# Cross-attention with a gate and RMS norm: the reciprocal root on GpSimd instead of VectorE

## Chip, core and metric

The kernel runs on one core of a Trainium2 chip. The metric is the time of one execution on the device in microseconds (us). The engines are called PE (TensorE, matrix products), DVE (VectorE), ACT (ScalarE), POOL (GpSimd) and SP (SyncE, which issues the DMAs).

## What is computed

For each of B = 8 sequences, with x of 512 x 512 and a memory of 1601 x 256:

```python
memory_proj = einsum('bme,de->bmd', memory, W_mem)
scores = einsum('bnd,bmd->bnm', x, memory_proj) / sqrt(D)          # D = 512
attn = softmax(scores, axis=-1)
memory_context = einsum('bnm,bmd->bnd', attn, memory_proj)
gate_input = concatenate([x, memory_context], axis=-1)
gate = sigmoid(einsum('bnf,df->bnd', gate_input, W_gate) + b_gate)
fused = x + gate * memory_context
out = fused * rsqrt(mean(square(fused), axis=-1) + 1e-6) * norm_w
```

Everything is float32. The last line is the one that the change touches: the factor `rsqrt(mean + eps)`, one number for each of the 512 rows of a sequence.

## The kernel before

**Tiling.** 512 rows of x are NT = 4 tiles of 128 rows; the 1601 rows of memory are MT = 13 tiles, the last of 65 rows. Every large product is done as three products of 32-bit parts (a "hi" and a "lo" part: hi·hi, hi·lo, lo·hi), so each operand tile is split: ACT copies the hi part (line 625), DVE subtracts it to get the lo part (line 828, the helper `lo_part`).

**Stages of one iteration b.** PE does the scores of sequence b (lines 353 to 355 with q and mt), then the gate and context products of sequence b-1, then the x half of the gate product of b, then the weighted sum of memory (lines 514 to 516), in the middle of which it computes the queries of b+1. ACT takes the exponential, the copies and the squares; DVE takes the maxima, the subtractions, the lo parts, the gate arithmetic and the stream transposes that prepare b+1. POOL only adds up the exponentials (`add_p`, line 1145): 12 additions of 128x512 in each iteration, into `psum_rows`.

**Order.** It is written out by hand, engine by engine, with semaphores between them; each engine runs its own list in order. A `wait_ge` holds up everything that stands behind it on its engine. Iteration 0 and iteration 7 are written out, 1 to 6 are a loop.

**The rows' factor.** ACT squares the four tiles of `fused` and leaves the sums in `sq_sum`, a 128x4 tile (line 700, semaphore `squares_done`). In iterations 1 to 7 DVE does `rms(b - 1)` after its last `p_lo`, then the four `output` operations (line 1010, 128x512 each) of sequence b-1, and then, for b+1, the lo parts `q_lo` and `mt_lo` (two each), and `u_lo` (two) of b itself. PE's first score product of b+1 waits for `q_lo` and `mt_lo`. In iteration 7 nothing is prepared: `u_lo` stands right behind the outputs, and PE's gate products of the last sequence wait for it. After that the last sequence is finished in a tail without overlap, with its own `rms(B - 1)`; there ACT (line 821) scales two tiles by `r_rms`, DVE the other two (lines 1125 and 1010), and SP stores them.

`rms` is a chain of 11 DVE operations on 128x4 tiles: the mean plus eps (line 996), a first guess from the bits of the number (line 997), and three Newton steps of three operations (lines 1000 to 1002). Each waits for the one before by the semaphore `newton`.

Of the kernel before, what the change touches and what calls it, by code (L numbers as in the profile page):

```python
# [37 lines left out]
P = 128  # L38
BLOCK = 32
BLOCKS = P // BLOCK  # L40
EPS = 1e-6

RSQRT_MAGIC = float(0x5F3759DF)
NEWTON_STEPS = 3


def xattn_kernel(nc: bass.Bass, x, mem, w, wg, b_gate, norm_w, out):
# [19 lines left out]
    with ExitStack() as ctx:  # L67
# [55 lines left out]
        sq_sum = sb("sq_sum", [P, NT])  # L123
        mean_sq = sb("mean_sq", [P, NT])
        r_rms = sb("r_rms", [P, NT])
        nw_a = sb("nw_a", [P, NT])
        nw_b = sb("nw_b", [P, NT])

        w_raw = x_again[:, :, :].rearrange("p a (k c) -> p (a k) c", c=C)
        wg_raw = [  # L130
# [53 lines left out]
        p_has_lo, xt_has_lo, q_has_lo = sem("p_has_lo"), sem("xt_has_lo"), sem("q_has_lo")  # L184
        u_has_lo, gx_done, r_first, r_done = sem("u_has_lo"), sem("gx_done"), sem("r_first"), sem("r_done")
        z_done, gated, fused_done = sem("z_done"), sem("gated"), sem("fused_done")
        newton, out_done = sem("newton"), sem("out_done")

        normed, tail_done = sem("normed"), sem("tail_done")

        p_added = sem("p_added")

        NEWTON_OPS = 2 + 3 * NEWTON_STEPS

        WT, WG2T, WG1T, V = range(0, 2), range(2, 6), range(6, 10), range(10, 12)

# [426 lines left out]
        def _(act):  # L623
# [192 lines left out]

            act.wait_ge(normed, NT - 1)

            act.wait_ge(newton, NEWTON_OPS * B)
            for j in range(1, NT - 1):  # L820
                nc.scalar.activation(fused[:, j, :], gate[:, j, :], ACT.Copy,
                                     scale=r_rms[:, j : j + 1]).then_inc(tail_done, 1)
# [3 lines left out]
        def _(dve):  # L826
# [154 lines left out]
                nc.vector.tensor_tensor(fused[:, j, :], fused[:, j, :], x_again[:, j % 2, :],  # L981
                                        ALU.add).then_inc(fused_done, 1)

            def rms(b):

                count = [NEWTON_OPS * b]

                def link(instruction):

                    count[0] = count[0] + 1  # L990
                    instruction.then_inc(newton, 1)
                    dve.wait_ge(newton, count[0])


                dve.wait_ge(squares_done, NT * (b + 1))
                link(nc.vector.tensor_scalar(mean_sq[:, :], sq_sum[:, :], 1.0 / D, EPS, ALU.mult, ALU.add))
                link(nc.vector.tensor_scalar(r_rms[:, :].bitcast(I32), mean_sq[:, :].bitcast(I32), -0.5, RSQRT_MAGIC,
                                             ALU.mult, ALU.add))
                for _ in range(NEWTON_STEPS):
                    link(nc.vector.tensor_tensor(nw_a[:, :], r_rms[:, :], mean_sq[:, :], ALU.mult))  # L1000
                    link(nc.vector.scalar_tensor_tensor(nw_b[:, :], nw_a[:, :], -0.5, r_rms[:, :], ALU.mult, ALU.mult))
                    link(nc.vector.scalar_tensor_tensor(r_rms[:, :], nw_b[:, :], 1.5, r_rms[:, :], ALU.add, ALU.mult))

            def scale_by_norm(j):

                dve.wait_ge(fused_done, NT * (B - 1) + j + 1)
# [17 lines left out]
            def iteration(b, first, last):  # L1024
# [12 lines left out]
                if first:  # L1037

                    dve.wait_ge(in_rows, 32)
                    reduce_max(b, first)  # L1040
                    for g in [*WG1T, V[0]]:
                        weights(g)
                    shift(b, 0)
                    shift(b, 1)
                    shift(b, 2)
                    for t in range(MT):
                        for q in SPLIT_BY_SOFTMAX.get(t, []):
                            mem_lo_part(b, q)
                        softmax(b, t, not last)
                        if t == 1:  # L1050
                            weights(V[1])
                        if 1 <= t < 1 + NT:
                            add_bias(b, t - 1, first)
                        transpose_next(b, t, first)
                else:
                    reciprocal(b - 1)
                    gate_input(b - 1, 0)
                    reduce_max(b, first)
                    gate_ctx(b - 1, 0)
                    gate_input(b - 1, 1)  # L1060
                    add_x(b - 1, 0)
                    shift(b, 0)
                    shift(b, 1)
                    shift(b, 2)
                    for t in range(MT):

                        if t in (1, 2):
                            gate_input(b - 1, t + 1)
                        if 3 <= t < 3 + NT:
                            add_bias(b, t - 3, first)  # L1070
                        if t in (0, 2, 4):
                            gate_ctx(b - 1, 1 + t // 2)
                        if t in ADD_AT:
                            add_x(b - 1, ADD_AT.index(t) + 1)
                        for q in SPLIT_BY_SOFTMAX.get(t, []):
                            mem_lo_part(b, q)
                        softmax(b, t, not last)
                        if not last:
                            transpose_next(b, t, first)
                    rms(b - 1)  # L1080
                    for j in range(NT):
                        output(b - 1, j)
                if not last:
# [36 lines left out]
            gate_ctx(B - 1, NT - 1)  # L1120
            add_x(B - 1, NT - 1)
            scale_by_norm(NT - 2)
            rms(B - 1)

            nc.vector.tensor_scalar(fused[:, 0, :], gate[:, 0, :], r_rms[:, 0:1], None, ALU.mult).then_inc(out_done, 1)
            output(B - 1, NT - 1)

# [2 lines left out]
        def _(pool):  # L1130
            def add_p(b, t, first):
# [12 lines left out]
                    a = psum_rows[0:r, :]  # L1144
                nc.gpsimd.tensor_tensor(psum_rows[0:r, :], a, p_tmp[0:r, t % TMP_RING, :], ALU.add).then_inc(p_added, 1)  # L1145

            nc.gpsimd.memset(ident[:, :], 0.0).then_inc(cleared, 1)
            pool.wait_ge(cleared, 1)
            nc.gpsimd.affine_select(out=ident[:, :], in_=ident[:, :], compare_op=ALU.not_equal, fill=1.0, base=0,
                                    pattern=[[-1, P]], channel_multiplier=1).then_inc(ready_ident, 1)  # L1150
# [2 lines left out]
            with pool.Fori(1, B) as b:  # L1153
                for t in range(1, MT):
                    add_p(b, t, False)


# [24 lines left out]
```

## Time and profile before

| what | us |
|---|---|
| median of 3 runs | 568.89 |
| lowest, highest | 568.46, 569.97 |
| span of the profiled execution | 567.1 |
| first to last score product of one loop iteration (148.48 to 215.53) | 67.05 |

The span is counted from the first to the last instruction on the engines; the run's time has 1.8 us more, which lie outside it. The page of the profile gives, for each engine, the busy time as a share of the span. PE's rows are modelled at their ends: a 128x512 product is shown as 0.39 us long, though the next one starts 0.23 us after it, so PE's pace is read from start to start. All times below are counted from the start of the span.

### The profile page before, as it was taken

Reading aid. Unit: us, or ns where it says so; the run is one execution under the profiler, and the core shown is the slowest. Engines: PE = TensorE matmul, PEld = TensorE weight load, DVE = VectorE, ACT = ScalarE, POOL = GpSimd, SP = SyncE. Lnnn points to the kernel's source line nnn. Section 1 sums busy time; section 2 is a strip of 40 time slices with the busy share of each in tenths; the row PEclk is TensorE's granted clock in tenths of the full one; section 3 lists DMA queues with packets and bytes.
Section 4 is the critical chain, followed back from the end, with each engine's and each line's share of the span. In section 5 each row is a group of like instructions: output and inputs, shape, how many; then the busy total and the mean of one; then the engine's idle time right before and its main releaser. Section 6 shows DMA issues by size and latency. Waiting matters only on the chain.

```text
span 567.1 us, 8588 instructions
## 1 busy us (share of the span) xinstructions
PE 541.8 (96%) x2416; PEld 436.3 (77%) x2416; DVE 511.6 (90%) x847; ACT 336.1 (59%) x633; POOL 134.2 (24%) x102
## 2 busy tenths in 40 slices
PE   6999999999999999999999999999999999999992
PEld 5877788877788777878788777887778777787882
DVE  3789959999899999899988998999988999889976
ACT  3666637665567655585466664666556754657534
POOL 0005500244002520055101550024300352005600
PEclk9999999999999999999999999999999999999997
DMA  9965151520853109521285115652095210210033
GB/s 235 271 102 113 52 134 42 99 69 26 186 137 93 37 3 237 102 74 37 83 176 102 55 37 146 130 98 78 1 214 125 77 37 33 97 33 29 1 113 111
DMA packets 89457, 54.24 MB, mean 96 GB/s; under 512 B 52696, under 2 KB 79840, under 8 KB 89440
## 3 DMA queue, kind: packets, MB, share of 16 engines
q1 hardware_dynamic: 89296, 53.51, 39.4%
q10 hardware_dynamic: 144, 0.52, 0.3%
q8 instruction: 8, 0.13, 0.1%
q14 instruction: 9, 0.07, 0.0%
HBM read 45.63 MB, written 8.39 MB: 95 GB/s over the span
## 4 chain that ended last, share of the span: by engine, by line
DVE 41%; PE 39%; issue 15%; ACT 2%; DMA 1%; DVEq 0%; ACTq 0%
PE bank L353 12%; DVE p_lo L828 11%; PE bank L355 11%; PE bank L354 11%; DVE s L869 6%; DVE bank L934 5%; DVE fused L974 3%; DVE gate L895 3%; DVE fused L981 2%; DVE xt_lo L828 2%; ACT fused L686 2%; DVE gate L924 2%; DVE fused L1010 1%; DVE q_lo L828 1%; PE bank L534 1%
## 5 line engine op out<-in xcount | busy, mean ns | idle before, releaser
L1145 POOL TENSOR_TENSOR psum_rows<-psum_rows,p_tmp 128x512 f32<-128x512 f32 (+1 forms) x88 | 122.6, 1393 | 94.1 <-ACT p_tmp L663 93.0
L828 DVE TENSOR_TENSOR p_lo<-p_tmp,p_hi 128x512 fp32r<-128x512 f32 (+1 forms) x104 | 92.4, 890 | 4.8 <-ACT p_hi L625 4.8
L663 ACT ACTIVATE p_tmp<-s 128x512 f32<-128x512 f32 (+1 forms) x104 | 65.3, 628 | 43.6 <-DVE s L869 43.0
L514 PE MATMUL bank<-p_hi,mem_hi 128*128 128x512 f32 (+1 forms) x208 | 81.8, 393 | 2.3 <-DVE p_lo L828 2.3
L1145 POOL TENSOR_TENSOR psum_rows<-p_tmp 128x512 f32<-128x512 f32 x8 | 10.8, 1354 | 308.7 <-ACT p_tmp L663 308.7
L353 PE MATMUL bank<-q_hi,mt_hi 128*128 128x512 f32 (+1 forms) x208 | 82.3, 396 | 1.1 <-DVE mt_lo L828 1.0
L355 PE MATMUL bank<-q_hi,mt_lo 128*128 128x512 f32 (+1 forms) x208 | 81.2, 390 | 0.0
L354 PE MATMUL bank<-q_lo,mt_hi 128*128 128x512 f32 (+1 forms) x208 | 81.2, 390 | 0.0
L515 PE MATMUL bank<-p_lo,mem_hi 128*128 128x512 f32 (+1 forms) x208 | 81.1, 390 | 0.0
L516 PE MATMUL bank<-p_hi,mem_lo 128*128 128x512 f32 (+1 forms) x208 | 80.9, 389 | 0.0
L625 ACT ACTIVATE s<-bank 128x512 f32<-128x512 f32 (+1 forms) x104 | 62.1, 597 | 22.0 <-PE bank L355 21.6
L869 DVE TENSOR_TENSOR s<-s,bank 128x512 f32<-128x512 f32 (+1 forms) x104 | 68.6, 673 | 0.0
L840 DVE TENSOR_TENSOR run<-run,s 128x512 f32<-128x512 f32 (+1 forms) x88 | 60.0, 681 | 8.0 <-ACT s L625 5.8
L625 ACT ACTIVATE p_hi<-p_tmp 128x512 fp32r<-128x512 f32 (+1 forms) x104 | 63.5, 617 | 0.0
L353 PE MATMUL bank<-wg1t_hi,xt_hi 128*128 128x512 f32 x128 | 51.9, 405 | 5.9 <-DVE gate L895 5.9
L354 PE MATMUL bank<-wg1t_lo,xt_hi 128*128 128x512 f32 x128 | 50.0, 391 | 0.0
L355 PE MATMUL bank<-wg1t_hi,xt_lo 128*128 128x512 f32 x128 | 49.9, 390 | 0.0
L514 PEld LDWEIGHTS bank<-p_hi,mem_hi 128*128 128x128 f32 (+1 forms) x208 | 39.0, 188 | 13.2 <-DVE p_lo L828 5.3
L353 PEld LDWEIGHTS bank<-q_hi,mt_hi 128*128 128x128 f32 (+1 forms) x208 | 38.2, 184 | 12.2 <-issue 3.1
L625 ACT ACTIVATE mt_hi<-bank 128x512 fp32r<-128x512 f32 (+1 forms) x56 | 30.2, 554 | 28.7 <-PE bank L355 28.7
L516 PEld LDWEIGHTS bank<-p_hi,mem_lo 128*128 128x128 f32 (+1 forms) x208 | 39.0, 188 | 8.3
L355 PEld LDWEIGHTS bank<-q_hi,mt_lo 128*128 128x128 f32 (+1 forms) x208 | 38.2, 184 | 9.2
(91 smaller groups left out, 1040.8 us busy)
## 6 DMA issues: line engine op xcount, KB each, us to landing
mem_raw<-in_ctx_dram SPq DMA_DIRECT2D x48, 256.0 KB, 2.9
mem_blocks<-in_ctx_dram SPq DMA_DIRECT2D x32, 272.0 KB
x_raw<-in_x_dram SPq DMA_DIRECT2D x32, 256.0 KB, 4.6
x_again<-in_x_dram SPq DMA_DIRECT2D x32, 256.0 KB, 2.8
out_dram<-fused SPq DMA_DIRECT2D x32, 256.0 KB, 2.1
mem_blocks<-in_ctx_dram SPq DMA_DIRECT2D x28, 128.0 KB, 5.5
gate<-in_L_xattn_W_gate_dram SPq DMA_DIRECT2D x2, 512.0 KB, 5.8
fused<-in_L_xattn_W_gate_dram SPq DMA_DIRECT2D x2, 512.0 KB, 7.4
```

Source lines behind the costliest of these rows:

```text
L353: nc.tensor.matmul(dst, a_hi, b_hi, start=(start and i == 0), stop=False)
L354: nc.tensor.matmul(dst, a_hi, b_lo, start=False, stop=False)
L355: last = nc.tensor.matmul(dst, a_lo, b_hi, start=False, stop=(stop and i == n - 1))
L514: nc.tensor.matmul(dst, mem_hi[0:r, t, cs], p_hi[0:r, t, :], start=(t == 0), stop=False)
L515: nc.tensor.matmul(dst, mem_hi[0:r, t, cs], p_lo[0:r, t % LO_RING, :], start=False, stop=False)
L516: last = nc.tensor.matmul(dst, mem_lo[0:r, t, cs], p_hi[0:r, t, :], start=False, stop=(t == MT - 1))
L625: return nc.scalar.activation(dst, src, ACT.Copy)
L663: nc.scalar.activation(p_tmp[0:r, t % TMP_RING, :], s[0:r, t, :], ACT.Exp, scale=float(D) ** -0.5).then_inc(exp_done, 1)
L828: return nc.vector.tensor_tensor(dst, src, hi.bitcast(F32), ALU.subtract)
L840: nc.vector.tensor_tensor(run[0:r, :], a, s[0:r, t, :], ALU.max).then_inc(run_done, 1)
L869: nc.vector.tensor_tensor(s[0:r, t, :], s[0:r, t, :], bank[MAX_BANK][0:r, :], ALU.subtract).then_inc(shifted, 1)
L1145: nc.gpsimd.tensor_tensor(psum_rows[0:r, :], a, p_tmp[0:r, t % TMP_RING, :], ALU.add).then_inc(p_added, 1)
```

## The change

The chain on DVE is taken out. POOL gets an `rms` of three operations on 128x4 tiles: `sq_sum` times a tile that holds 1/D, plus a tile that holds eps, to the power of a tile that holds -0.5. Each waits for the one before (`mean_done`, `guarded`), and the last one counts up `rms_done`. It stands on POOL behind the twelve `add_p` of iterations 1 to 7, and once more at the end. DVE waits for `rms_done` where its chain stood, in front of the outputs, and ACT waits for `rms_done` in the tail. The three constant tiles are filled by POOL at the start, between the clearing of `ident` and the `affine_select` that makes it the identity.

```diff
-            def rms(b):
-                count = [NEWTON_OPS * b]
-                def link(instruction):
-                    count[0] = count[0] + 1
-                    instruction.then_inc(newton, 1)
-                    dve.wait_ge(newton, count[0])
-                dve.wait_ge(squares_done, NT * (b + 1))
-                link(nc.vector.tensor_scalar(mean_sq[:, :], sq_sum[:, :], 1.0 / D, EPS, ALU.mult, ALU.add))
-                link(nc.vector.tensor_scalar(r_rms[:, :].bitcast(I32), mean_sq[:, :].bitcast(I32), -0.5, RSQRT_MAGIC,
-                                             ALU.mult, ALU.add))
-                for _ in range(NEWTON_STEPS):
...
@@ DVE, iteration b @@
-                    rms(b - 1)
+                    dve.wait_ge(rms_done, b)
                     for j in range(NT):
                         output(b - 1, j)
@@ DVE, tail @@
-            rms(B - 1)
+            dve.wait_ge(rms_done, B)
@@ ACT, tail @@
-            act.wait_ge(newton, NEWTON_OPS * B)
+            act.wait_ge(rms_done, B)
@@ POOL @@
+            def rms(b):
+                pool.wait_ge(squares_done, NT * (b + 1))
+                nc.gpsimd.tensor_tensor(mean_sq[:, :], sq_sum[:, :], one_in_d[:, :], ALU.mult).then_inc(mean_done, 1)
+                pool.wait_ge(mean_done, b + 1)
+                nc.gpsimd.tensor_tensor(mean_sq[:, :], mean_sq[:, :], eps_rows[:, :], ALU.add).then_inc(guarded, 1)
+                pool.wait_ge(guarded, b + 1)
+                nc.gpsimd.tensor_tensor(r_rms[:, :], mean_sq[:, :], minus_half[:, :], ALU.pow).then_inc(rms_done, 1)
             nc.gpsimd.memset(ident[:, :], 0.0).then_inc(cleared, 1)
+            nc.gpsimd.memset(minus_half[:, :], -0.5).then_inc(ready_half, 1)
+            nc.gpsimd.memset(one_in_d[:, :], 1.0 / D).then_inc(ready_half, 1)
+            nc.gpsimd.memset(eps_rows[:, :], EPS).then_inc(ready_half, 1)
+            pool.wait_ge(ready_half, 3)
...
             with pool.Fori(1, B) as b:
                 for t in range(1, MT):
                     add_p(b, t, False)
+                rms(b - 1)
+            rms(B - 1)
```

On DVE, at the end of a loop iteration, this stood in a row before (the register steps compute the loop's semaphore values; the first rows are the last preparation for b+1 and the last `p_lo`):

```order
L950 STREAM_TRANSPOSE bank<-mem_blocks 128x512
L828 TENSOR_TENSOR p_lo<-p_tmp,p_hi 65x512
L996 TENSOR_SCALAR mean_sq<-sq_sum 128x4
L992 ISA
L997 TENSOR_SCALAR r_rms<-mean_sq 128x4
L992 REGISTER_ALU
L1000 TENSOR_TENSOR nw_a<-r_rms,mean_sq 128x4
L992 REGISTER_ALU
L1001 SCALAR_TENSOR_TENSOR nw_b<-nw_a,r_rms 128x4
L992 REGISTER_ALU
L1002 SCALAR_TENSOR_TENSOR r_rms<-nw_b,r_rms 128x4
L992 REGISTER_ALU
```

and this stands at the same place now:

```order
L948 STREAM_TRANSPOSE bank<-mem_blocks 128x512
L826 TENSOR_TENSOR p_lo<-p_tmp,p_hi 65x512
L988 SCALAR_TENSOR_TENSOR fused<-fused,r_rms,norm_rows 128x512 x4
L903 ISA
L826 TENSOR_TENSOR q_lo<-bank,q_hi 128x512
L903 REGISTER_ALU
L826 TENSOR_TENSOR q_lo<-bank,q_hi 128x512
L842 ISA
L826 TENSOR_TENSOR mt_lo<-bank,mt_hi 128x512
```

The eleven operations between the last `p_lo` and the four outputs are gone, and nothing else moved on DVE (its line numbers are smaller by 2 to 22).

On POOL, at the end of a loop iteration, this stood before:

```order
L1145 TENSOR_TENSOR psum_rows<-psum_rows,p_tmp 65x512
L1153 REGISTER_ALU
L1153 COMPARE_AND_BRANCH
L67 UNCONDITIONAL_BRANCH
```

and this stands there now, with the copy for the last sequence behind the loop's branch:

```order
L1124 TENSOR_TENSOR psum_rows<-psum_rows,p_tmp 65x512
L1128 REGISTER_ALU
L1129 TENSOR_TENSOR mean_sq<-sq_sum,one_in_d 128x4
L1131 TENSOR_TENSOR mean_sq<-mean_sq,eps_rows 128x4
L1133 TENSOR_TENSOR r_rms<-mean_sq,minus_half 128x4
L1145 REGISTER_ALU
L1145 COMPARE_AND_BRANCH
L1129 TENSOR_TENSOR mean_sq<-sq_sum,one_in_d 128x4
L1131 TENSOR_TENSOR mean_sq<-mean_sq,eps_rows 128x4
L1133 TENSOR_TENSOR r_rms<-mean_sq,minus_half 128x4
L65 UNCONDITIONAL_BRANCH
```

The three small operations came in behind the last addition of the iteration; no addition moved.

## Rows read from the trace of the kernel before

**Rows 1.** The page, part 1: busy us (share of the span) xinstructions.

```profile
PE 541.8 (96%) x2416; PEld 436.3 (77%) x2416; DVE 511.6 (90%) x847; ACT 336.1 (59%) x633; POOL 134.2 (24%) x102
```

**Rows 2.** Waits: engine line waited for: us in total, times, longest us.

```profile
PE bank L353 <- DVE mt_lo L828: 1.0, 5, 0.2
...
PEld bank L353 <- DVE mt_lo L828: 0.6, 1, 0.6
```

**Rows 3.** Timeline of PE at two turns: start, length, instruction [idle before <-releaser].

```profile
81.29 0.39 PE L516 MATMUL bank<-p_hi,mem_lo 65*128 65x512 f32 x1
81.52 0.40 PE L353 MATMUL bank<-q_hi,mt_hi 128*128 128x512 f32 x1
...
147.87 0.39 PE L516 MATMUL bank<-p_hi,mem_lo 65*128 65x512 f32 x1
148.48 0.49 PE L353 MATMUL bank<-q_hi,mt_hi 128*128 128x512 f32 x1 [0.21 <-DVE mt_lo L828]
148.81 0.40 PE L354 MATMUL bank<-q_lo,mt_hi 128*128 128x512 f32 x1
```

**Rows 4.** Timeline of DVE before the second turn.

```profile
141.07 0.66 DVE L828 TENSOR_TENSOR p_lo<-p_tmp,p_hi 65x512 fp32r<-65x512 f32 x1
141.66 0.14 DVE L996 TENSOR_SCALAR mean_sq<-sq_sum 128x4 f32<-128x4 f32 x1
...
143.81 2.74 DVE L1010 SCALAR_TENSOR_TENSOR fused<-fused,r_rms,norm_rows 128x512 f32<-128x512 f32 x4
...
147.66 1.28 DVE L828 TENSOR_TENSOR mt_lo<-bank,mt_hi 128x512 fp32r<-128x512 f32 x2
```

**Rows 5.** Timeline of ACT, same stretch.

```profile
140.51 0.19 ACT L700 ACTIVATION_READ_ACCUMULATOR squares_out<-fused 128x1 f32 x1
...
144.69 1.08 ACT L625 ACTIVATE mt_hi<-bank 128x512 fp32r<-128x512 f32 x2
```

**Rows 6.** Timelines of ACT, POOL and DVE: POOL's last addition of iteration 1.

```profile
135.93 0.63 ACT L663 ACTIVATE p_tmp<-s 65x512 f32<-65x512 f32 x1
...
136.72 1.45 POOL L1145 TENSOR_TENSOR psum_rows<-psum_rows,p_tmp 65x512 f32<-65x512 f32 x1 [0.88 <-ACT p_tmp L663]
...
137.53 1.19 DVE L828 TENSOR_TENSOR p_lo<-p_tmp,p_hi 128x512 fp32r<-128x512 f32 x1
```

**Rows 7.** Timeline of the start; then POOL's additions by line: duration ns min/median/max.

```profile
0.35 0.10 POOL L1170 MEMSET const-uint8-127<- 128x1 uint8 x1
...
1.19 0.29 POOL L1149 TENSOR_SCALAR_AFFINE_SELECT ident<-ident 128x128 f32<-128x128 f32 x1 [0.24 <-POOL ident L1147]
...
5.26 3.66 PE L364 MATMUL bank<-ident,x_raw 128*128 128x128 f32 x16 [5.26 <-DMA x_raw<-in_x_dram]
...
L1145 POOL TENSOR_TENSOR psum_rows<-psum_rows,p_tmp x88: 1286/1329/1796, 48.0 to 536.3; 128x512 f32<-128x512 f32 x80, 65x512 f32<-65x512 f32 x8
```

**Rows 8.** Timelines of DVE, ACT and PE at the end of iteration 7.

```profile
538.82 1.28 DVE L828 TENSOR_TENSOR p_lo<-p_tmp,p_hi 128x512 fp32r<-128x512 f32 x2
...
539.47 0.19 ACT L700 ACTIVATION_READ_ACCUMULATOR squares_out<-fused 128x1 f32 x1
...
542.19 2.74 DVE L1010 SCALAR_TENSOR_TENSOR fused<-fused,r_rms,norm_rows 128x512 f32<-128x512 f32 x4
...
543.81 1.29 ACT L625 ACTIVATE u_hi<-bank 128x512 fp32r<-128x512 f32 x2 [4.15 <-PE bank L516]
...
544.30 0.95 PE L449 MATMUL bank<-ones,psum_rows 128*128 128x1 f32 x8
545.59 0.50 PE L353 MATMUL bank<-v_hi,u_hi 128*128 128x512 f32 x1 [0.34 <-DVE u_lo L828]
```

**Rows 9.** Timeline of the tail.

```profile
559.59 0.19 ACT L700 ACTIVATION_READ_ACCUMULATOR squares_out<-fused 128x1 f32 x1
559.81 0.17 DVE L996 TENSOR_SCALAR mean_sq<-sq_sum 128x4 f32<-128x4 f32 x1 [0.19 <-ACT squares_out L700]
...
562.05 1.33 ACT L821 ACTIVATE fused<-gate,r_rms 128x512 f32<-128x512 f32 x2 [2.27 <-DVE r_rms L1002]
```

More of the change, by code:

```diff
@@ L41 @@
 EPS = 1e-6
-RSQRT_MAGIC = float(0x5F3759DF)
-NEWTON_STEPS = 3
 def xattn_kernel(nc: bass.Bass, x, mem, w, wg, b_gate, norm_w, out):
@@ L125, in xattn_kernel @@
         r_rms = sb("r_rms", [P, NT])
-        nw_a = sb("nw_a", [P, NT])
-        nw_b = sb("nw_b", [P, NT])
+        minus_half = sb("minus_half", [P, NT])
+        one_in_d = sb("one_in_d", [P, NT])
+        eps_rows = sb("eps_rows", [P, NT])
         w_raw = x_again[:, :, :].rearrange("p a (k c) -> p (a k) c", c=C)
@@ L186, in xattn_kernel @@
         z_done, gated, fused_done = sem("z_done"), sem("gated"), sem("fused_done")
-        newton, out_done = sem("newton"), sem("out_done")
+        mean_done, guarded, rms_done, out_done = sem("mean_done"), sem("guarded"), sem("rms_done"), sem("out_done")
+        ready_half = sem("ready_half")
         normed, tail_done = sem("normed"), sem("tail_done")
         p_added = sem("p_added")
-        NEWTON_OPS = 2 + 3 * NEWTON_STEPS
         WT, WG2T, WG1T, V = range(0, 2), range(2, 6), range(6, 10), range(10, 12)
@@ L982, in add_x @@
                                         ALU.add).then_inc(fused_done, 1)
-            def rms(b):
-                count = [NEWTON_OPS * b]
-                def link(instruction):
-                    count[0] = count[0] + 1
-                    instruction.then_inc(newton, 1)
-                    dve.wait_ge(newton, count[0])
-                dve.wait_ge(squares_done, NT * (b + 1))
-                link(nc.vector.tensor_scalar(mean_sq[:, :], sq_sum[:, :], 1.0 / D, EPS, ALU.mult, ALU.add))
-                link(nc.vector.tensor_scalar(r_rms[:, :].bitcast(I32), mean_sq[:, :].bitcast(I32), -0.5, RSQRT_MAGIC,
-                                             ALU.mult, ALU.add))
-                for _ in range(NEWTON_STEPS):
-                    link(nc.vector.tensor_tensor(nw_a[:, :], r_rms[:, :], mean_sq[:, :], ALU.mult))
-                    link(nc.vector.scalar_tensor_tensor(nw_b[:, :], nw_a[:, :], -0.5, r_rms[:, :], ALU.mult, ALU.mult))
-                    link(nc.vector.scalar_tensor_tensor(r_rms[:, :], nw_b[:, :], 1.5, r_rms[:, :], ALU.add, ALU.mult))
             def scale_by_norm(j):
```

## Prediction

> **What bounds the kernel now.** I read the page first. PE is busy for 96% of the span and DVE for 90% [rows 1]. With two engines so full, taking work off DVE pays only where DVE releases PE, so I looked next at the list of waits for PE waiting on what stands behind the chain. PE's first score product waits for DVE's `mt_lo` at six turns of the iteration: five times in the list as a product, once as its weight load [rows 2]. These are the six turns from iteration 1 on to 7. The turn from iteration 0 to 1 has no chain before it, and there PE goes from the last weighted product to the first score product in 0.23 us, its ordinary pace [rows 3]. At the next turn, where DVE has done its chain, the same step takes 0.61 us and the following one 0.33 (the first product after a pause is slow), so 0.94 instead of 0.46: **0.48 us lost at each of six turns** [rows 3].
>
> The timeline of DVE shows why. The chain runs from 141.66 to 143.81, 2.15 us; from there on outputs, `q_lo` and `mt_lo` follow without idle time, and the first half of `mt_lo` is what PE waits for [rows 4]. DVE comes too late by 0.4 us only, however: what the chain costs PE at a turn is less than a quarter of its length.
>
> The chain stands at two more places. In iteration 7, `u_lo` behind the outputs releases PE, which waits 0.34 us [rows 8]. In the tail nothing covers it: from the end of the squares (559.78) to ACT's first use of the factor (562.05) are 2.27 us [rows 9].
>
> **What the change removes.** At eight places a chain of about 2.15 us on DVE. At the six turns at most 0.48 us of it can be won. ACT is no obstacle: `mt_hi` is done at 145.77, earlier than `mt_lo` would start even if it moved up by 1.8 us [rows 4, 5].
>
> **What it adds: POOL's three operations.** No row shows a small arithmetic operation on POOL, so I bound each. Below: filling a 128x1 tile took 0.10 us. Above, for the multiplication and the addition: the `affine_select` on 128x128, a 32 times larger tile, took 0.29 us [rows 7]. I take 0.20 for each, the middle. The gap between two dependent POOL operations was 0.24 us before that `affine_select` [rows 7]; I take 0.20, since a part of it belongs to the start. From the end of an ACT operation to a POOL operation that waits for it pass 0.16 us (136.56 to 136.72) [rows 6]; I use 0.15.
>
> The power is the unknown of this case. POOL has no operation of this kind in the trace. Below it is no shorter than the filling, 0.10. Above, the nearest row is the largest that POOL has, 1.80 us for an addition of 128x512 [rows 7], 128 times as many elements; a power computed in software may cost many times an addition for each element, so this end isn't safe. Between ends so far apart I take the geometric middle, sqrt(0.10 x 1.80) = 0.42, say **0.44 us**, and keep d for it.
>
> **The shared port.** DVE's `p_lo` of 0.66 us takes 1.19 when POOL's addition is running, and ends 0.55 after that addition ends (138.17 to 138.72): it has waited for POOL, not been slowed by it [rows 4, 6]. In the Trainium skill, "SBUF — State Buffer", section "Who interferes with whom", an operation of VectorE with two SBUF inputs and a GpSimd operation that reads SBUF exclude each other; by that rule, the trace agrees. So POOL's small operations can also wait for `p_lo`, and I count this against the change.
>
> **When the factor is ready, at a turn.** Squares end at 140.70 [rows 5]. POOL's additions of this iteration ended at 138.17 [rows 6], so POOL is free. Multiplication from 140.85 to 141.05. The addition could start at 141.25, but `p_lo` holds the port until about 141.66 [rows 4]: 141.66 to 141.86. Power from 142.06, end 142.06 + d, DVE starts 0.10 later. With d = 0.44 the outputs start at 142.60 instead of 143.81, **1.21 us earlier**; without the port 0.41 more. The turn needs only 0.48. So each turn wins min(0.48, 1.65 - d) = 0.48, in sum **2.88 us**. What is late next there is PE itself, which has its own weighted products until then. Downstream nothing new comes up: the scores are paced by PE, and the softmax stage starts from PE's transposes, so the whole iteration shifts.
>
> **Iteration 7.** Squares end at 539.66, `p_lo` holds the port until about 540.08 [rows 8]. Multiplication to 540.28, addition to 540.68, power from 540.88, outputs at 540.98 + d = 541.42 instead of 542.19: 0.77 us. PE can use 0.34, since its row sums last until 545.25, and `u_hi` is ready then [rows 8]: **0.34 us**.
>
> **Tail.** 559.78 + 0.15 + 0.20 + 0.20 + 0.20 + 0.20 = 560.73 for the start of the power, then d and 0.10 to ACT: 561.27 instead of 562.05 [rows 9], **0.78 us** (1.32 with all durations at their lower ends and gaps unchanged).
>
> **Start.** Three more fillings on POOL, 0.10 us each, at most 0.3 us before the identity. The identity was ready at 1.48 and PE's first transpose waited for x until 5.26 [rows 7]: hidden by 3.8 us of DMA, nothing.
>
> **Sum:** 2.88 + 0.34 + 0.78 = 4.00 us off the profiled span of 567.1. The median stands 1.8 us above that span and I carry this over: 568.89 - 4.0 = **564.9 us**.
>
> **As a function of d:** six turns of min(0.48, 1.65 - d), iteration 7 with min(0.34, 1.21 - d), the tail with 1.22 - d. The gain falls under 0.3% of the time (1.7 us, about what a measurement of this kernel can tell from no change) at d = 1.33, is zero at 1.54, and is a loss of 1.7 us at 1.75. Beyond, every us of d costs 8 us.
>
> **Rivals.**
> - **The power is slow.** DVE then sits in front of its outputs, with `q_lo`, `mt_lo` and `u_lo` queued behind, and PE waits for these. The place is the same eight waits; it decides from d = 1.54 on. At the upper end from rows, d = 1.80: 6 x 0.15 + 0.59 + 0.58 = 2.1 us lost, 571.0 us. For it speaks that no row bounds a power on POOL; against it, that there are only four elements in a partition.
> - **The turns don't pay.** PE starts the scores earlier, and the softmax stage, where DVE is full, gives it back by a longer wait. DVE's own work after the turn is not shortened, and its 90% speak for it; that PE releases the reduction at that stage's head speaks against it. Then only 0.34 + 0.78 remain: 567.8 us, within 0.3%.
> - **The first power loads code.** No row shows POOL loading code: the accumulating additions, from the first at 48.0 us on, lie between 1286 and 1796 ns [rows 7], which speaks against it; but none of them is a power. If the first power took the 1.8 us of my upper end and the others 0.44, the first turn would lose 0.15 instead of gaining 0.48: 565.5 us. The Trainium skill, "GPSIMD Engine Reference", section "2.1 Instruction dispatch", states about 6 us for the first call into freshly loaded code; by an estimate from that page the first turn would be late by 4.7 us and the time 570.1. No run here shows such a load.
>
> **How the numbers follow.** The power below 1.33 us and the turns paying: 0.64, all of it faster by over 0.3%. The turns don't pay: 0.13, within. A first power that costs several us once: 0.03, within. The power above 1.33: 0.20, of which 0.05 lie between 1.33 and 1.75, within, and 0.15 above, slower. So faster 0.64, same 0.21, slower 0.15. Low end: all of POOL at its lower bounds gives 4.00 + 0.54 = 4.5, with the runs' spread below the median (0.4) 563.9, say 563.8. High end: 571.0, the power at 1.80; above it lie about 0.14.
>
> **What would show it right or wrong.** The power's row, below 1.3 us; DVE's idle time before the first output, about 142.6 - 141.7 = 0.9 us a turn, released by POOL; PE from last weighted to first score product in 0.23 us at all seven turns, and no wait for `mt_lo`; a loop iteration of 66.6 instead of 67.05 us; the tail from squares to ACT's scaling 1.5 us. Wrong: a wait of DVE for POOL above 2.15 us, or PE's turns closed with the iteration still at 67.05.

## The result, and the profile after

The changed kernel takes 565.17 us (median of 4 runs, 564.69 to 565.91) against 569.43 us for the kernel before beside it (4 runs, 568.46 to 571.36): a ratio of 0.9918 with a 95% interval of 0.9896 to 0.9941. The prediction said 564.9 in a range of 563.8 to 571.0, faster. The profiled execution of the changed kernel has a span of 564.0 us.

The page after (line numbers are 2 to 22 smaller than before on the engines). First part 1, then part 4, the shares of the chain that ended last:

```profile
PE 540.6 (96%) x2416; PEld 436.7 (77%) x2416; DVE 499.7 (89%) x759; ACT 336.1 (60%) x633; POOL 152.5 (27%) x129
...
PE 55%; DVE 29%; issue 12%; ACT 2%; DMA 1%; DVEq 0%; ACTq 0%; POOLq 0%; POOL 0%
```

DVE has 88 operations less, PE the same work as in [rows 1]. PE now holds 55% of the chain, where the page of before had DVE 41% and PE 39%.

The waits of the changed kernel (engine line waited for: us in total, times, longest us). These are three of those that are new; PE's wait for `mt_lo` of [rows 2] isn't in the list any more:

```profile
POOL mean_sq L1129 <- ACT squares_out L698: 33.1, 8, 17.9
...
DVE fused L988 <- POOL r_rms L1133: 8.7, 7, 1.5
...
ACT fused L819 <- POOL r_rms L1133: 1.7, 1, 1.7
```

A turn is the step from one iteration's last weighted product on PE to the first score product of the next. The second one that has a factor before it, for each engine of the changed kernel (start, length, instruction [idle before <-releaser]):

```profile
207.80 0.20 POOL L1129 TENSOR_TENSOR mean_sq<-sq_sum,one_in_d 128x4 f32<-128x4 f32 x1 [2.60 <-ACT squares_out L698]
208.08 0.74 POOL L1131 TENSOR_TENSOR mean_sq<-mean_sq,eps_rows 128x4 f32<-128x4 f32 x1
208.90 1.03 POOL L1133 TENSOR_TENSOR r_rms<-mean_sq,minus_half 128x4 f32<-128x4 f32 x1
...
208.10 0.66 DVE L826 TENSOR_TENSOR p_lo<-p_tmp,p_hi 65x512 fp32r<-65x512 f32 x1
209.97 2.74 DVE L988 SCALAR_TENSOR_TENSOR fused<-fused,r_rms,norm_rows 128x512 f32<-128x512 f32 x4 [1.21 <-POOL r_rms L1133]
...
214.91 0.39 PE L514 MATMUL bank<-p_hi,mem_lo 65*128 65x512 f32 x1
215.14 0.40 PE L351 MATMUL bank<-q_hi,mt_hi 128*128 128x512 f32 x1
215.37 0.40 PE L352 MATMUL bank<-q_lo,mt_hi 128*128 128x512 f32 x1
```

Read it beside [rows 3] and [rows 4]. From the start of the last `p_lo` to the outputs pass 1.87 us instead of 2.74, though DVE stands idle for 1.21 of them. PE goes on in 0.23 + 0.23 us, its pace, where it took 0.61 + 0.33 before. The three POOL operations take 0.20, 0.74 and 1.03 us, and DVE's idle time of 1.21 us is what the prediction put at 0.9.

The end of the chain in the tail, to be read beside [rows 9]:

```profile
557.06 0.19 ACT L698 ACTIVATION_READ_ACCUMULATOR squares_out<-fused 128x1 f32 x1
557.32 0.20 POOL L1129 TENSOR_TENSOR mean_sq<-sq_sum,one_in_d 128x4 f32<-128x4 f32 x1 [17.92 <-ACT squares_out L698]
557.60 0.20 POOL L1131 TENSOR_TENSOR mean_sq<-mean_sq,eps_rows 128x4 f32<-128x4 f32 x1
557.88 1.01 POOL L1133 TENSOR_TENSOR r_rms<-mean_sq,minus_half 128x4 f32<-128x4 f32 x1
...
558.98 1.33 ACT L819 ACTIVATE fused<-gate,r_rms 128x512 f32<-128x512 f32 x2 [1.74 <-POOL r_rms L1133]
```

From the end of the squares (557.25) to ACT's scaling are 1.73 us instead of 2.27.

So that the start of a run, where the arrival of x moves everything by a few tenths, doesn't enter, the table counts from the first score product of iteration 1 (81.52 before, 81.81 after). "Six turns" is the stretch from there to iteration 7's first score product, six loop iterations with their turns.

| stretch, us | before | after | won |
|---|---|---|---|
| six turns (iterations 1 to 6) | 402.23 | 399.89 | 2.34 |
| iteration 7, to the gate products of the last sequence | 61.84 | 61.32 | 0.52 |
| squares of the last tile to the scaling | 2.27 | 1.73 | 0.54 |
| first score product of iteration 1 to the end | 485.6 | 482.2 | 3.4 |

The start took 0.29 us longer in the profiled execution of the changed kernel, and 3.4 - 0.3 = 3.1 is the difference of the spans. PE's first transposes waited for x until 5.42 instead of 5.26, not for the identity.

### The profile page after: what moved, and what is told of

It is laid out like the page before. It is cut to its first block, busy times and chain, and to the rows that moved or that the text cites. A ratio compares the mean times of both kernels' runs of the same rounds, so it can differ in the third digit from the quotient of the medians.

```text
span 564.0 us, 8469 instructions
## 1 busy us (share of the span) xinstructions
PE 540.6 (96%) x2416; PEld 436.7 (77%) x2416; DVE 499.7 (89%) x759; ACT 336.1 (60%) x633; POOL 152.5 (27%) x129
## 4 chain that ended last, share of the span: by engine, by line
PE 55%; DVE 29%; issue 12%; ACT 2%; DMA 1%; DVEq 0%; ACTq 0%; POOLq 0%; POOL 0%
PE bank L351 14%; PE bank L353 13%; PE bank L352 13%; DVE p_lo L826 7%; DVE s L867 5%; DVE bank L932 5%; PE bank L512 4%; PE bank L513 3%; PE bank L514 3%; DVE fused L972 3%; DVE gate L893 2%; DVE xt_lo L826 2%; ACT fused L684 2%; DVE gate L922 2%; DVE fused L979 2%
## 5 line engine op out<-in xcount | busy, mean ns | idle before, releaser
L1124 POOL TENSOR_TENSOR psum_rows<-psum_rows,p_tmp 128x512 f32<-128x512 f32 (+1 forms) x88 | 126.0, 1432 | 94.2 <-ACT p_tmp L661 93.1
```

## The experiments

**Theory:** what counts is only the moment at which the factor is ready, at six turns with a cap (PE's own pace), in iteration 7 and in the tail. **Rivals:** the relief of VectorE's busy time pays, wherever the factor is computed; GpSimd's added operations take part of the gain back; the tail carries nearly everything. Each run was measured beside the kernel before on the same chip; there were two chips, so that runs are compared by their ratio or by their traces. "To the end" is the stretch of the last line of the table above, in the profiled execution.

### A later factor

```diff
+                nc.gpsimd.tensor_tensor(r_first_pow[:, :], mean_sq[:, :], minus_half[:, :], ALU.pow).then_inc(pow_once, 1)
+                pool.wait_ge(pow_once, b + 1)
                 nc.gpsimd.tensor_tensor(r_rms[:, :], mean_sq[:, :], minus_half[:, :], ALU.pow).then_inc(rms_done, 1)
```

> The changed kernel with the power computed twice in a row, the second waiting for the first, at all eight places. In the changed kernel's trace the power takes 1.02 us and the gap before it 0.08, so the factor is 1.10 us later. Theory (only the moment at which the factor is ready counts): from the start of the last p_lo to the outputs 1.86 + 1.10 = 2.96 us at a turn, where the chain on VectorE needed 2.74; PE waits for mt_lo again, 0.2 us a turn longer than before the change; 0.5 us are lost in iteration 7 and 0.56 in the tail. In sum 2.4 us slower than the kernel before, about 571.8, that is 6.6 above the changed kernel. Rival (relief of VectorE's busy time is what pays, since VectorE has no more work than in the changed kernel): within 1 us of the changed kernel's 565.2 but for the tail, so below 567.5.

Measured: 571.14 us against 569.23, ratio 1.0027 (1.0014 to 1.0041). With 1.1 us more of a wait on an engine that is three quarters idle, the whole gain is gone and more. The six turns take 403.52 us, 1.29 more than before (0.2 a turn expected), and PE takes 0.81 us from the last weighted to the first score product. The waits in its trace:

```profile
DVE fused L989 <- POOL r_rms L1136: 16.3, 7, 2.6
...
PE bank L352 <- DVE mt_lo L827: 2.4, 6, 0.4
```

DVE has exactly the work of the changed kernel here and the result is slower than the kernel before, so the relief of DVE isn't what pays: that rival falls. To the end, this profiled execution lost 3.9 us, 1.5 more than the theory's 2.4; that part has another cause, at the end of this document. In the medians the loss is 1.9.

### Loop or tail alone

Set against the changed kernel, both put VectorE's chain of 11 operations back at one kind of place; GpSimd's operations for that place are taken out.

```diff
@@ GpSimd in the iterations only: DVE, tail @@
-            dve.wait_ge(rms_done, B)
+            rms(B - 1)
@@ GpSimd in the tail only: DVE, iteration b @@
-                    dve.wait_ge(rms_done, b)
+                    rms(b - 1)
```

> GpSimd's three operations in iterations 1 to 7, VectorE's chain in the tail. Theory: the tail falls back from 1.73 to 2.27 us between the squares and the scaling, 0.54 us above the changed kernel, about 565.7; 3.7 us faster than before. Rival (most of the gain is in the exposed tail and the turns give theirs back in the softmax stage): about 568.

> VectorE's chain in iterations 1 to 7, GpSimd's three operations in the tail alone. Theory: 0.54 us faster than the kernel before, about 568.9, with PE waiting for mt_lo at the turns as before. Rival (the tail carries the gain): about 566.

Measured: in the iterations only 565.46 us (ratio 0.9931, 0.9909 to 0.9952), in the tail only 568.97 (0.9999, 0.9984 to 1.0015). To the end they won 3.2 and 0.4 us; together that is 3.6, where the change won 3.4. Turns in the iterations only: 399.59 us; in the tail only: 402.30, as before. The gain sits where PE waited for `mt_lo`. That the tail carries it is refuted.

### No factor at all

This kernel leaves the factor out: `r_rms` is filled with 1 once at the start, and nobody computes it or waits for it.

```diff
-                    dve.wait_ge(rms_done, b)
+                    dve.wait_ge(squares_done, NT * b)
...
-                rms(b - 1)
-            rms(B - 1)
```

> The changed kernel without the factor: it is a constant 1, nobody computes it and nobody waits for it; the rest is unchanged. It shows what is to be had at all. Theory: a turn can win no more than 0.48 us, iteration 7 no more than 0.34, the tail 2.2: 5.4 us under the kernel before, about 564.0, so only some 1.3 us under the changed kernel, nearly all of it in the tail. Rival (VectorE's readiness still holds back the turns of the changed kernel, or GpSimd's small operations disturb it through the shared port): further 0.1 us a turn or more, 563.3 or lower, and a loop iteration under 66.6 us.

Measured: 563.52 us, ratio 0.9895 (0.9874 to 0.9916). The six turns take 399.54 us: **the floor of a loop iteration with its turn is 66.59 us**, and the change, at 66.65, is all but on it. 0.44 us is what it can win over 67.04, and not 0.48: PE's step from the last weighted to the first score product was 0.61 us only at the turn of [rows 3], and at the six turns 0.61, 0.60, 0.58, 0.56, 0.57 and 0.52. The last of them, in the kernel before:

```profile
483.23 0.39 PE L516 MATMUL bank<-p_hi,mem_lo 65*128 65x512 f32 x1
483.75 0.50 PE L353 MATMUL bank<-q_hi,mt_hi 128*128 128x512 f32 x1
```

Against the pace of 0.23 that is 2.06 us in sum, 0.34 a turn. The 0.10 of a first product after a pause falls into the stretch of the six turns five times, 0.5 us; the sixth stands in the line of iteration 7. Together 2.6 us, where this run won 2.69. To the end 5.4 us are won, 2.0 more than by the change, most of it in the tail, where the scaling follows the squares without a wait.

### A shorter chain, left on VectorE

```diff
-NEWTON_STEPS = 3
+NEWTON_STEPS = 2
```

> The kernel before with two Newton steps instead of three, all on VectorE, GpSimd without the new work: a shorter chain, 8 operations of 0.197 us instead of 11, 0.59 us less. The factor is a little less exact. Theory (only the moment at which mt_lo is ready counts, whoever computes the factor): PE was late by 0.38 us at a turn, 0.59 covers that, so the six turns win what the run without a factor won, 0.44 us each; iteration 7 wins 0.34, the tail 0.59: 3.6 us faster than before, about 565.6, the same as the move to GpSimd. Rival (the work has to leave VectorE): 3/11 of the chain goes, so about 3/11 of the gain, near 568.2.

Measured: 565.04 us, ratio 0.9922 (0.9906 to 0.9938), as the change. Turns 399.62, to the end 3.7 us won. Cutting 0.59 us of 2.15 won everything that the turns had to give: PE was late by 0.38 us. This is the strongest run for the theory. Nothing left DVE here, and the rival's 568.2 is missed by 3 us.

### What the added operations cost others

VectorE's chain stays in use, and POOL does its three operations besides, into tiles of its own that nobody reads. DVE's wait for them stands behind the outputs.

```diff
                     for j in range(NT):
                         output(b - 1, j)
+                    dve.wait_ge(rms_done, b)
...
                 add_p(b, t, False)
+                rms(b - 1)
+            rms(B - 1)
```

> The kernel before, VectorE's chain in use, and GpSimd's three operations done besides into tiles that nobody reads. Measures what the added operations cost others by themselves. Theory: at most 0.1 us a turn by the shared port, 0 to 0.6 us slower than before, iteration 67.05 to 67.15 us. Rival (the added operations disturb VectorE by more, and this ate a part of the gain): 1.5 us or more slower.

Measured: 569.34 us, ratio 1.0004 (0.9991 to 1.0018); turns 402.28 us against 402.23. The operations cost others nothing that shows, though the second one waits itself for DVE's `p_lo`:

```profile
274.75 0.20 POOL L1157 TENSOR_TENSOR pm_sq<-sq_sum,one_in_d 128x4 f32<-128x4 f32 x1 [2.60 <-ACT squares_out L706]
275.03 0.74 POOL L1159 TENSOR_TENSOR pm_sq<-pm_sq,eps_rows 128x4 f32<-128x4 f32 x1
275.85 1.03 POOL L1161 TENSOR_TENSOR pr_rms<-pm_sq,minus_half 128x4 f32<-128x4 f32 x1
```

### The price of a power

```diff
+            for i, (n, op) in enumerate(((4, ALU.add), (4, ALU.pow), (4, ALU.pow), (1, ALU.pow), (16, ALU.pow), (64, ALU.pow), (64, ALU.add))):
+                nc.gpsimd.tensor_tensor(probe_o[:, 0:n], probe_a[:, 0:n], probe_e[:, 0:n], op).then_inc(probe, 1)
+                pool.wait_ge(probe, 3 + i)
```

> The changed kernel with a probe at the start, where GpSimd is idle: an addition on 128x4, then powers on 128x4, 128x4 again, 128x1, 128x16 and 128x64, then an addition on 128x64, each waiting for the one before. The time of the whole says nothing. If the power's cost is fixed for an instruction, all powers take about 1.0 us. If it goes by the element: 0.2 + 0.2 for each column, so 0.4 on 128x1, 1.0 on 128x4, 3.5 on 128x16, 13 on 128x64. If the first power loads code, the first of the two on 128x4 is longer than the second by a microsecond or more.

One execution, the profiled one (564.94 us). POOL's timeline in its first microseconds, cut at the probe's single operations (the longer rows of a view merge operations that follow one another):

```profile
1.85 0.20 POOL L1148 TENSOR_TENSOR probe_o<-probe_a,probe_e 128x4 f32<-128x4 f32 x1
2.13 1.02 POOL L1148 TENSOR_TENSOR probe_o<-probe_a,probe_e 128x4 f32<-128x4 f32 x1
...
2.13 2.11 POOL L1148 TENSOR_TENSOR probe_o<-probe_a,probe_e 128x4 f32<-128x4 f32 x2
...
4.95 2.91 POOL L1148 TENSOR_TENSOR probe_o<-probe_a,probe_e 128x16 f32<-128x16 f32 x1
...
7.93 10.55 POOL L1148 TENSOR_TENSOR probe_o<-probe_a,probe_e 128x64 f32<-128x64 f32 x1
```

and its groups by shape, where the power on 128x1 stands alone:

```profile
L1148 POOL TENSOR_TENSOR probe_o<-probe_a,probe_e 128x1 f32<-128x1 f32 x1 | 0.5, 548 | 0.1
```

The addition on 128x4 takes 0.20 us. The first power takes 1.02, and the second of the pair ends 2.11 us after the first began, so it takes 1.0 as well: no loading of code shows. Powers on 1, 4, 16 and 64 columns take 0.55, 1.02, 2.91 and 10.55 us. Between 1 and 64 columns that is 10.0 / 63 = 0.16 us a column, and 0.39 us whatever the width. By the column both expected pictures were off: a fixed price is refuted, and the slope is 0.16, not 0.2, above a larger base.

### Versions that beat both

Two operations instead of three, and then also the tail's factor in two parts, the first three tiles ahead of the last:

```diff
-                nc.gpsimd.tensor_tensor(mean_sq[:, :], sq_sum[:, :], one_in_d[:, :], ALU.mult).then_inc(mean_done, 1)
-                pool.wait_ge(mean_done, b + 1)
-                nc.gpsimd.tensor_tensor(mean_sq[:, :], mean_sq[:, :], eps_rows[:, :], ALU.add).then_inc(guarded, 1)
+                nc.gpsimd.tensor_tensor(mean_sq[:, :], sq_sum[:, :], eps_rows[:, :], ALU.add).then_inc(guarded, 1)
...
-            nc.gpsimd.memset(eps_rows[:, :], EPS)
+            nc.gpsimd.memset(eps_rows[:, :], D * EPS)
...
+                    nc.vector.tensor_scalar(norm_rows[:, :], norm_rows[:, :], float(D) ** 0.5, None, ALU.mult)
# split tail
+            dve.wait_ge(rms_done, B + 1)
             output(B - 1, NT - 1)
...
-            rms(B - 1)
+            for i, c in enumerate((slice(0, NT - 1), slice(NT - 1, NT))):
+                pool.wait_ge(squares_done, NT * (B - 1) + c.stop)
+                nc.gpsimd.tensor_tensor(mean_sq[:, c], sq_sum[:, c], eps_rows[:, c], ALU.add).then_inc(guarded, 1)
+                pool.wait_ge(guarded, B + i)
+                nc.gpsimd.tensor_tensor(r_rms[:, c], mean_sq[:, c], minus_half[:, c], ALU.pow).then_inc(rms_done, 1)
```

> The changed kernel, improved: 1/D is folded into norm_w (times sqrt(D), once at the start) and D*eps into the constant, so the mean needs no multiplication and two operations are left; in the tail the factors of the first three tiles are computed before the last tile's squares are done, and the last one alone afterwards. Theory: the turns are at their floor and win nothing; the tail's last output ends 1.45 + 0.75 us after the squares instead of 1.73 + 1.33: 0.86 us faster than the changed kernel, about 564.3. Rival (the end is set by the stores or by POOL, not by the factor): the same as the changed kernel.

> The changed kernel once more, beside the two improved ones on the same chip. 0.992 of the time before, 565 to 565.6.

> The changed kernel with two operations on GpSimd instead of three (1/D folded into norm_w, D*eps into the constant), the tail not split. Theory: the turns are at their floor; the tail ends 0.28 us earlier (one operation of 0.20 and one gap of 0.08): 0.3 us under the changed kernel. Rival (the turns still have something to win): 0.5 us or more.

> Two operations and the split tail once more, beside the changed kernel on the same chip. 0.9 to 1.2 us under the changed kernel, as between the earlier runs.

| kernel | median us | ratio to before, interval | six turns | to the end, won |
|---|---|---|---|---|
| changed, again | 565.00 | 0.9916, 0.9897 to 0.9935 | 399.71 | 3.6 |
| two operations | 563.96 | 0.9906, 0.9886 to 0.9926 | 399.48 | 4.1 |
| two operations, split tail | 563.99 | 0.9906, 0.9888 to 0.9924 | 399.65 | 4.7 |
| the same, second time | 563.88 | 0.9900, 0.9880 to 0.9920 | 399.63 | 4.8 |

The split tail is 1.1 to 1.2 us under the change in the trace and 1.0 to 1.1 in the median (0.86 expected; 0.80 of it are the tail, the rest is spread). The first of the split tail's two rows was measured on the other chip than the three other rows. Two operations alone are 0.5 under the change in the trace: 0.28 are the tail (1.46 us instead of 1.74 of waiting), 0.23 the turns, which vary by as much; in the median it is 1.0, more than the 0.3 expected, and part of that is its start (first score product of iteration 1 at 80.54 instead of 81.37). The split tail:

```profile
555.74 1.18 POOL L1153 TENSOR_TENSOR r_rms<-mean_sq,minus_half 128x3 f32<-128x3 f32 x1
556.18 0.19 ACT L698 ACTIVATION_READ_ACCUMULATOR squares_out<-fused 128x1 f32 x1
556.89 0.18 POOL L1151 TENSOR_TENSOR mean_sq<-sq_sum,eps_rows 128x1 f32<-128x1 f32 x1
...
557.01 1.33 ACT L819 ACTIVATE fused<-gate,r_rms 128x512 f32<-128x512 f32 x2 [0.65 <-POOL r_rms L1153]
557.16 0.69 POOL L1153 TENSOR_TENSOR r_rms<-mean_sq,minus_half 128x1 f32<-128x1 f32 x1
...
557.88 0.75 DVE L988 SCALAR_TENSOR_TENSOR fused<-fused,r_rms,norm_rows 128x512 f32<-128x512 f32 x1 [0.44 <-POOL r_rms L1153]
```

The last squares end at 556.37 and the last output 2.26 us later, as expected (2.20); ACT scales its two tiles in the meantime. The first power is still running when the last squares are done, and holds the second one's operations up by 0.4 to 0.5 us.

### Why the kernel before varies more

The median won 4.3 us, the span of the profiled executions 3.1. All 10 runs of the changed kernel lie between 564.22 and 565.91; the kernel before, in its many runs beside the experiments, between 568.05 and 571.49, and its profiled execution (567.1, so 568.9) stands in the lower half. The mean granted clock of each execution, on record for the 68 of the kernel before beside the experiments, divides them:

| mean granted clock | executions | median us | lowest, highest |
|---|---|---|---|
| 0.992 | 31 | 570.3 | 569.54, 571.49 |
| 0.993 to 0.996 | 37 | 568.85 | 568.05, 569.87 |

So most of the one-sided spread goes with the clock: the second group spreads over 1.8 us, as the changed kernel does (1.7), and that kernel has no execution at 0.992. The last run moves one output behind the two `u_lo` in iteration 7, to test what may bring the lower clock:

```diff
-                    for j in range(NT):
+                    for j in range(NT - 1 if last else NT):
                         output(b - 1, j)
...
+                if last:
+                    output(b - 1, NT - 1)
```

> The kernel before, with its chain on VectorE at all places, and only this moved: in iteration 7 the fourth output stands behind the two u_lo instead of in front. u_lo is then ready as early as u_hi allows and PE pauses no longer before the gate products of the last sequence; the turns and the tail stay as they were. Theory A: only the pause goes, 0.3 to 0.5 us. Theory B: in about half the executions of the kernel before the pause is followed by some microseconds at the lower of TensorE's two clocks (the executions with a mean granted clock of 0.992 are 1 to 2 us longer than those with 0.994), and with the pause this goes too: 1.0 to 1.3 us off the median, no execution at 0.992 and none above 569.5. By A alone the executions stay spread up to 571.

Measured: 568.67 us against 568.95, ratio 0.9987 (0.9976 to 0.9999). The pause is gone (PE starts the gate products 0.88 us after its row sums began, in [rows 8] it was 1.29). None of its 12 executions has the mean clock 0.992, which 4 of the 17 beside it have. One is at 570.06 all the same, and the 1.0 to 1.3 us of theory B aren't in the median; with only 4 of 17 at the lower clock beside it, the median before, 568.95, had little of it to lose. By this run alone B is not settled. The other runs speak for it: among the executions whose clock is on record, 41 of the 104 of kernels that pause there (before, power twice, tail only, both chains) are at 0.992 or below, and none of the 58 of kernels without this pause. Against it stands that the tail-only kernel, which pauses as the kernel before does, has one in 12. Only the power-twice kernel was profiled with such a stretch (at the end of this document).

The profiled execution of this last run shows a second cause that neither theory had. The turn from iteration 1 to 2:

```profile
136.59 3.21 POOL L1147 TENSOR_TENSOR psum_rows<-psum_rows,p_tmp 65x512 f32<-65x512 f32 x1 [0.89 <-ACT p_tmp L663]
...
137.41 0.66 DVE L828 TENSOR_TENSOR p_lo<-p_tmp,p_hi 128x512 fp32r<-128x512 f32 x1
138.62 1.72 DVE L981 TENSOR_TENSOR fused<-fused,x_again 128x512 f32<-128x512 f32 x1
...
147.74 0.39 PE L516 MATMUL bank<-p_hi,mem_lo 65*128 65x512 f32 x1
148.90 0.49 PE L353 MATMUL bank<-q_hi,mt_hi 128*128 128x512 f32 x1 [0.77 <-DVE mt_lo L828]
```

In [rows 6] the addition was done after 1.45 us and `p_lo`, which began 0.81 us after it, waited for it and took 1.19. Here `p_lo` began 0.82 us after the addition and went through in 0.66; the addition lasted 3.21 us, and the next DVE operation with two SBUF inputs waited 1.1 us for its end. DVE lost 0.5 us, and PE took 1.16 us for the step at the turn instead of 0.61. At three turns of the six the last addition was longer than 1.9 us and PE's step too long (1.16, 1.10 and 1.08 us): 1.6 us in sum. In the changed kernel's profile the last addition was long three times too (2.00, 3.20 and 2.64 us). The second of them:

```profile
270.38 3.20 POOL L1124 TENSOR_TENSOR psum_rows<-psum_rows,p_tmp 65x512 f32<-65x512 f32 x1 [0.90 <-ACT p_tmp L661]
...
272.40 1.73 DVE L979 TENSOR_TENSOR fused<-fused,x_again 128x512 f32<-128x512 f32 x1
...
281.57 0.39 PE L514 MATMUL bank<-p_hi,mem_lo 65*128 65x512 f32 x1
281.81 0.49 PE L351 MATMUL bank<-q_hi,mt_hi 128*128 128x512 f32 x1
282.14 0.39 PE L352 MATMUL bank<-q_lo,mt_hi 128*128 128x512 f32 x1
```

and cost 0.1 us there, a first product of 0.33 instead of 0.23. The 0.87 us by which DVE is earlier cover 0.38 of lateness and the 0.5 of the lost race.

A long addition isn't always dear, though. The kernel with GpSimd in the tail only has one of 2.63 us, and PE's step at the turn that follows is 0.60 us, as at its other turns:

```profile
202.96 2.63 POOL L1149 TENSOR_TENSOR psum_rows<-psum_rows,p_tmp 65x512 f32<-65x512 f32 x1 [0.90 <-ACT p_tmp L666]
...
204.97 1.18 DVE L984 TENSOR_TENSOR fused<-fused,x_again 128x512 f32<-128x512 f32 x1
...
214.11 0.39 PE L519 MATMUL bank<-p_hi,mem_lo 65*128 65x512 f32 x1
214.71 0.49 PE L356 MATMUL bank<-q_hi,mt_hi 128*128 128x512 f32 x1 [0.21 <-DVE mt_lo L831]
```

What counts is the row of the DVE operation that waits. In all 14 traces, at the last addition of iterations 1 to 6, it is 1.16 to 1.20 us long when the addition takes 1.45 or 2.64, and 1.72 to 1.75 us when it takes 2.0 or 3.2: DVE waits 0.5 or 1.1 us, and its row ends 0.55 us after the addition's each time. The longer wait is there at 9 of these 84 turns, three of them in the last run and none in the profiled execution of the kernel before.

The widths of the runs fit this in part: the kernels whose PE waits for `mt_lo` spread over 1.9 (power twice), 3.6 (tail only), 2.7 (both) and 2.5 us (this one), those with slack there over 0.4 to 1.7 (0.4 iterations only, 0.7 no factor, 1.2 two Newton steps, 1.4 two operations, 1.7 the changed kernel). The first four have 12 executions each and the others 6 to 10, which alone makes a range wider. The tail-only kernel reaches 571.20 at a mean clock of 0.993, so the clock isn't all of it there; how often an execution loses the race wasn't measured beyond the one profiled of each kernel.

## Why the prediction was right

**What bounds.** Right. PE's lateness of 0.38 us at the turn and the cap of 0.48 a turn were read from PE's start-to-start times [rows 3]; the run with two Newton steps and the one without a factor reached a floor of 66.6 us a loop iteration, from either side. The turns won 0.39 us each, 2.34 in sum, where 2.88 was said. One turn had been read for all six, and it was the latest of them: the lateness is 0.34 us on average, not 0.38, and one of the six slow first products falls into the line of iteration 7. That makes 2.6 of the 2.88. The remaining 0.2 went with the long additions, which used up the slack at two turns (first products of 0.33 us); these weren't in the sum.

**The power.** This is the term that was mis-sized: 1.02 us, where 0.44 was taken. It lay between the bounds 0.10 and 1.80. The forecast stood all the same, since by its own function the turns are at their cap up to d = 1.17. Half a microsecond more of power would have used up the slack: the outputs came 0.87 us earlier, and PE needed 0.38 of it.

**The gaps and small operations.** 0.20 us for the multiplication and the addition was right (0.20, 0.20 in the tail). The gap between dependent operations was 0.08, not 0.20. In the tail the errors partly cancel: the power is 0.57 longer, two gaps 0.24 shorter, POOL's start after ACT 0.08 shorter: 1.73 us where 1.49 was said, a gain of 0.54 instead of 0.78.

**The port.** Right, and at each of the six turns: the second operation takes 0.74 to 0.76 us instead of 0.20, ending 0.06 us after `p_lo` (208.82 and 208.76). Outputs were said to start 1.21 us earlier with d = 0.44; by its function, 1.65 - d, the power of 1.02 would give 0.63, and 0.87 was measured, the difference being the shorter gaps and the addition's early end behind `p_lo`, 0.06 us instead of 0.20.

**Iteration 7.** 0.52 us where 0.34 was said. 0.41 of it is at the place itself: PE goes on 0.88 us after the start of its row sums, where it was 1.29, and the prediction let them hold it up for 0.95. The other 0.11 is the faster first score product of iteration 7, the sixth of the turns' 0.10.

**Sum and median.** 3.4 us of 4.0 came in the trace. The medians moved by more, 4.3: of the four executions before, two (569.97 and 571.36) lie higher than any of the 37 at the higher mean clock. Against the median of those 37, 568.85, the ten executions of the changed kernel win 3.8 us. That this kernel would have none at the lower clock wasn't seen beforehand. The hit at 564.9 is in part luck: the sum was 0.6 us too large, and the changed kernel's profiled execution, 565.91, is the slowest of its four, so that the median, 565.17, came nearer to the forecast than the trace.

**Rivals.** The slow power was the right one to fear: at 1.02 + 1.10 (power twice) the kernel is 1.9 us slower than before. The formula with d = 2.12 gave 6 x 0.47 + 0.91 + 0.90 = 4.6; the shorter gaps make it less. The turns paid. No loading of code shows: in the probe the first and the second power take the same.

## What to carry to other kernels

Before moving work off a full engine, measure by how much the engine that waits for it is late: here 0.38 us of a chain of 2.15 decided nearly everything, and three ways of taking 0.6 to 2.15 us out of the chain (another engine, a shorter formula, nothing at all) came out within 0.1 us a turn of each other. A step that is late by a little also passes on every small disturbance; slack of half a microsecond nearly made the lost races disappear. Read every turn of a loop before multiplying: one read for six made the sum 0.2 us too large. And an exposed tail is worth splitting: what can be computed for the first tiles need not wait for the last.

## What the runs showed of the hardware

**A power on GpSimd** took 0.39 us and 0.16 us for each column of 128 in the probe (0.55, 1.02, 2.91 and 10.55 us for 1, 4, 16 and 64 columns), where an addition on 4 columns took 0.20. In the split tail, with DVE at work beside it, 3 columns took 1.18 us and 1 column 0.69, more than the 0.87 and 0.55 of that formula; the cause wasn't traced. A dependent POOL operation started 0.08 us after the one before, and POOL's multiplication 0.07 us after the squares, where an addition started 0.16 us after the exponential.

**At the shared port DVE loses 0.5 or 1.1 us, and which of the two isn't seen in the start times; nor is the longer addition always the dearer one.** An addition that begins 0.81 or 0.82 us ahead of `p_lo` gave one time 1.45 us with `p_lo` waiting 0.5, the other time 3.21 us with `p_lo` going through and the next operation with two SBUF inputs waiting 1.1; one of 2.63 us cost DVE 0.5 as well, one of 2.00 us in the changed kernel cost it 1.1. In the Trainium skill, "SBUF — State Buffer", section "Who interferes with whom", the shared port pair is an exclusive lock, and the order of issue decides who blocks. That the one waits for the other's end agrees with the traces (at all 84 turns of the 14 traces the waiting DVE row ends 0.55 us after the addition's); the order of issue does not show in them, since the addition's row begins first each time. POOL's rows may begin before the port is asked for; that wasn't measured.

**A pause of PE can be followed by the lower clock.** With the power computed twice, PE stood 0.84 us for `u_lo` after its row sums. The products that follow, and the clock in this stretch (PE, PEld, DVE, ACT and POOL busy, then the granted clock):

```profile
546.81 0.50 PE L352 MATMUL bank<-v_hi,u_hi 128*128 128x512 f32 x1 [0.84 <-DVE u_lo L827]
...
548.21 0.63 PE L354 MATMUL bank<-v_hi,u_lo 128*128 128x512 f32 x1
548.63 0.63 PE L352 MATMUL bank<-wt_hi,u_hi 128*128 128x512 f32 x1
...
546.50:550.00 3.50, 3.19 (x10) 2.53 (x11) 1.87 (x5) 0.34 (x1) 0.00 (x0) 0.70 0.88 294
```

From 547.85 to 551.19 products start every 0.36 to 0.43 us instead of 0.23: PE is at 1.2 GHz, the lower of its two levels (granted clock 0.52 from 547.8 to 551.2), for 3.3 us, and eight products cost 0.2 us more each. That makes up the 1.5 us more that this execution lost. Its mean granted clock is 0.989, and four more of that kernel's 12 executions are at 0.989 or 0.992. The mean also counts the tail, where the clock falls once PE has nothing to do and costs nothing (0.50 from 563 us on, in this execution as in the profiled one of the kernel before). In the profiled execution of the kernel before, with a wait of 0.34 us, the granted clock is full there. By an estimate from these rows, 3.3 us at half the clock lower the mean of an execution by 0.003 and cost it 1.6 us, about what divides the two groups of the kernel before (0.992 against 0.993 to 0.996, 1.4 us). No execution of that kernel at 0.992 was profiled, so that it is the same stretch there is not shown.
